# History attention: the reciprocal deviation spread by two single-pass products, and later waits at the history's end

## The chip, the cores and the metric

The kernel runs on one core of a Trainium2 chip. The metric is the device time of one execution in microseconds (us). TensorE multiplies matrices, VectorE (DVE), ScalarE (ACT) and GpSimd (POOL) work elementwise, SyncE (SP) issues the DMAs. Each engine runs its own instruction list in order and waits on semaphores for the others.

## The reference

Two transformer-like layers on x (128 tokens by 256 features). The first block looks at a history of 12544 tokens of 256 features. For each history token it computes

    h  = tok @ hist_W + hist_b              (512 features)
    hn = (h - mean(h)) * rsqrt(var(h) + 1e-5) * g + beta
    e  = gelu(hn)
    logit = gelu(e @ W1 + b1) @ W2 + b2

and then one context vector, the softmax(logit)-weighted sum of e over all tokens. From this vector come 3x3 kernels (one set for each of 16 heads), which are applied to the 128x128 score maps of x. Linear attention, a mixture of experts, a cross attention of x over the same 12544 tokens (keys and values are projections of the history), a retention block and a low-rank feed-forward part follow, one after the other.

## The kernel before, in words

**The history loop.** The 12544 tokens go through in 49 chunks of 256 (`NCH`, `CH`); features lie on partitions, tokens on columns. In one pass of its loop TensorE does, in this order: `project(n, 0)` (12 products of 256 columns), `mean_square(n-1)`, `values_turn(n-1)`, `project(n, 1)` (12 more), `spread_rstd(n-1)`, in odd passes `weight_logit`, `weight_hidden`, and `keys_product(n)` (12 products). The projections split each float32 number in a rounded part and a rest, both of type float32r, and sum three products; such a product is one record in the trace. A product of plain float32 operands is two records.

**The deviation.** The mean over features is taken out by centred weights, so only the variance is missing. ACT squares the 512 projected features, DVE adds them up to 128 partitions (`add_squares`), and `mean_square` (L673) sums the partitions by two products of one column each, whose stationary operand is the 128x128 block of squares. The result has tokens on partitions, two columns. DVE adds epsilon (`variance`, L1555), POOL raises to the power -0.5 (`deviation`, L1478, gives `h_rstd`, 128x2). `spread_rstd` (L681) turns this into a row that all partitions share: two plain float32 products, stationary operand a column of `h_rstd` broadcast to 128x128, moving operand the identity (128 columns). ACT copies the 256 columns out (`widen`, L1238, `rstd_wide`), and DVE's `normalise` (L1570) multiplies by it.

**DVE's order in a pass** (L1612 and after): `keys_parts(n-1)` (waits for ACT's `k_full`), `variance(n-1)`, in even passes `logit`, then from the 17th pass on a wait for POOL's `h_rs` and one `weighted_sum` (L1594), `normalise`, `add_squares(n)`, `normalise`.

**The history's end.** After the last pass DVE finishes the weighted sums and writes the context vector (`cc_wide`). Meanwhile TensorE turns xn (L769) and multiplies it by the query, key and value weights (`qkv0`), then waits for `cc_wide` and does `kg1` (four products of 256 columns and a bias of one row), then the 16 score products (`scores0`, L797), then turns `kg_h` (L803), from which the kernels come. Right behind `cc_wide`, DVE waits until the last key and value stores have landed and sets `history_done` (L1676). Three things wait for that: SP, before it loads `rows0` and the four pieces of FFN weights (L583, L586); ACT, before it copies `kT0` and `v0` (L1330, L1331); and, in order behind it, DVE's own `q_blocks` (L1699). The score products need `q_blocks` and `kT0`. `stay_awake(n, at)` (L756) issues n plain float32 products of the identity with itself into a bank nobody reads.

Of the kernel before, what the change touches and what calls it, by code (L numbers as in the profile page):

```python
# [19 lines left out]
F32 = mybir.dt.float32  # L20
F32R = mybir.dt.float32r
U8 = mybir.dt.uint8
U32 = mybir.dt.uint32
ALU = mybir.AluOpType
# [3 lines left out]
P = 128  # L28
# [12 lines left out]
NCH = S // CH  # L41
HB = CH // 2
# [33 lines left out]
VG = -(-TILES // VT)  # L76
# [29 lines left out]
def wait_at(eng, sem, value):  # L106

    if isinstance(value, int) and value <= 0:
        return
    eng.wait_ge(sem, value)  # L110
# [67 lines left out]
POOL_STEPS = """  # L178
half_power v_ones rstd1 rstd_kg rstd2 rstd_att rstd3 rstd4 turned5 rstd5 rms5 rstd6"""
DVE_STEPS = """  # L180
hist_constants hist_weights x_parts mask var1 xn1 g_shift cc_wide history_done q_blocks0 var_kg kg_n att0_0 att0_1
kg_hT att0_2 att0_3 kern_shift kernels s_max0 s_max2 s_max1 probT0 s_max3 probT1
probT2 s_max4 probT3 probT4 o0 o0T x1 var2 xn2 xT2 v1
kv_blocks var_att gated1 gT x2 var3 xn3 xT3 g_neg hid0 hid1 mixed0 hid2 mixed1 hid3 mixed2 hid4 mixed3 x3 var4
# [81 lines left out]
def build_kernel(nc, k_scratch, v_scratch, ones_scratch, ctx_t, x_in, mask_in, const_in, hist_in, l0_in, rows0_in, xw_in, x_bo_in, x_o_in, l1_in, rows1_in, v_in,  # L266
                 tables_in, out):
    with ExitStack() as outer:
        def sem(name):
            return outer.enter_context(nc.semaphore(name))  # L270

        def sb(name, shape, dt=F32, scope=outer):
            return scope.enter_context(nc.sbuf_tensor(name, shape, dt))


        bank = outer.enter_context(nc.psum_tensor("bank", [P, 8, 512], F32))
# [19 lines left out]
        ident = part(const, CONST_COLS, "ident")  # L296
# [19 lines left out]
        la = ExitStack()  # L316
# [13 lines left out]
        square1 = sb("square1", [P, CH], scope=la)  # L330
        h_var = sb("h_var", [P, 2], scope=la)
        h_rstd = sb("h_rstd", [P, 2], scope=la)
        rstd_wide = sb("rstd_wide", [P, CH], scope=la)
        normed = sb("normed", [P, 2, CT, PW], scope=la)
        eh = sb("eh", [P, 2, CT, GW], scope=la)
# [7 lines left out]
        cc_wide = k_full[:, NCH % 2].rearrange("p m (c t) -> p (m c) t", t=P)  # L343
# [11 lines left out]
        gone = sb("gone", [P, 1], scope=lb)  # L355
# [7 lines left out]
        kg_n = sb("kg_n", [P, D], scope=lb)  # L363
# [97 lines left out]
        ld_const, ld_hist, ld_small = sem("ld_const"), sem("ld_hist"), sem("ld_small")  # L461
# [4 lines left out]
        pe_s = Steps(sem("pe_steps"), PE_STEPS)  # L466
# [5 lines left out]
        h_high, h_low, h_proj, h_sq = sem("h_high"), sem("h_low"), sem("h_proj"), sem("h_sq")  # L472
        h_add2, h_add1, h_ms, h_ve, h_rs = sem("h_add2"), sem("h_add1"), sem("h_ms"), sem("h_ve"), sem("h_rs")
        h_bc, h_rw, h_nm, h_eh = sem("h_bc"), sem("h_rw"), sem("h_nm"), sem("h_eh")
        h_w1, h_hid, h_w2, h_lg = sem("h_w1"), sem("h_hid"), sem("h_w2"), sem("h_lg")
        h_gm, h_p, h_ws = sem("h_gm"), sem("h_p"), sem("h_ws")

# [32 lines left out]
        k_stored = [sem("k_stored0"), sem("k_stored1")]  # L510
        v_stored = [sem("v_stored0"), sem("v_stored1")]
# [131 lines left out]
        def _(pe):  # L643
# [31 lines left out]
                last.then_inc(h_ms, 1)  # L675

            def spread_rstd(n):
                pe.wait_ge(h_rs, n + 1)
                wait_at(pe, h_rw, n)
                for s in range(2):  # L680
                    last = nc.tensor.matmul(bank[:, 4, s * HB:(s + 1) * HB], h_rstd[:, s:s + 1].broadcast_to([P, P]),  # L681
                                            ident, start=True, stop=True)
                last.then_inc(h_bc, 1)

            def weight_hidden(i, part_of):
# [79 lines left out]
            def turn(name_in, src, name_out, at=0, banks=None):  # L765

                dve_s.wait(pe, name_in)
                for k in range(KD):
                    last = nc.tensor.transpose(bank[:, at, k * P:(k + 1) * P], src[:, k * P:(k + 1) * P], ident)  # L769
                pe_s.done(last, name_out)  # L770
# [6 lines left out]

            pe.wait_ge(ld_l0, 16 * L0_PIECES)
            pe.wait_ge(h_nm, CT * NCH)
            turn("xn1", xn, "xn1_t")  # L780
            act_s.wait(pe, "xT1")
            wq, wk, wv = (part(w0, L0_COLS, n, KD) for n in ("x_q", "x_k", "x_v"))
# [4 lines left out]


            pe.wait_ge(ld_kg, 16)
            dve_s.wait(pe, "cc_wide")  # L790
            kg1, kg2 = part(w0, L0_COLS, "kg1", CT), part(w0, L0_COLS, "kg2", KD)
            pe_s.done(product(bank[:, 0, 0:D], [(cc_wide[:, c], kg1[:, c]) for c in range(CT)]
# [3 lines left out]
            for h in range(H):  # L796
                last = nc.tensor.matmul(bank[:, 4 + h // 4, (h % 4) * T:(h % 4 + 1) * T], q_blocks[:, h // 8, h % 8],  # L797
                                        kT[:, h // 8], start=True, stop=True)
# [87 lines left out]
            for m in range(KD):  # L886
                nc.tensor.matmul(bank[:, 5, m * P:(m + 1) * P], k_sig[:, m * P:(m + 1) * P], v_lin[:, m * P:(m + 1) * P],
                                 start=True, stop=True)
# [617 lines left out]
        def _(dve):  # L1506
            V = nc.vector
            own = [0]

            def link(ins):  # L1510

                own[0] += 1
                ins.then_inc(dve_own, 1)
                dve.wait_ge(dve_own, own[0])

            def done(ins, name):

                dve_s.done(ins, name)
                dve_s.wait(dve, name)
# [3 lines left out]
            V.memset(ones[:, :], 1.0).then_inc(dve_own, 1)  # L1523
            V.memset(group_stats[:, :, :], 0.0).then_inc(dve_own, 1)
            own[0] += 3
            done(V.memset(inv_width[:, :], 1.0 / C2), "hist_constants")
            dve.wait_ge(ld_hist, 32)
            link(V.tensor_reduce(w_mean[:, :], w_raw, AX_X, ALU.add))
# [23 lines left out]
            def variance(n):  # L1552
                dve.wait_ge(h_ms, n + 1)
                wait_at(dve, h_rs, n)
                V.tensor_scalar(h_var[:, :], bank[:, 4, CH:CH + 2], LN_EPS, None, ALU.add).then_inc(h_ve, 1)  # L1555

            def add_squares(n):
                dve.wait_ge(h_sq, 2 * n + 2)
# [16 lines left out]
            def logit(i):  # L1575
                group, at, width = group_of(i), i % GP * PW, pair_width(i)
                gb = i // GP % 2
                dve.wait_ge(h_w2, i + 1)
                if i % GP == 0 and i >= 2 * GP:
                    dve.wait_ge(h_ws, pieces_before((i // GP - 1) * GC))  # L1580
                    dve.wait_ge(h_gm, i // GP - 1)
                V.tensor_scalar(logits[:, gb, at:at + width], bank[:, 6, 0:width], v_hist["b2"], None, ALU.add,
                                ALU.max, accum_out=pair_max[:, gb, i % GP:i % GP + 1]).then_inc(h_lg, 1)
                if i == pairs_of(group)[-1]:
                    dve.wait_ge(h_lg, i + 1)
                    V.tensor_reduce(group_stats[:, group, MAX_COL:MAX_COL + 1],
                                    pair_max[:, gb, pairs_of(group)[0] % GP:i % GP + 1], AX_X,
                                    ALU.max, negate=True).then_inc(h_gm, 1)

            def weighted_sum(group, half, c, lo, width):  # L1590
                gb = GROUPS[group][0] // GC % 2
                dve.wait_ge(h_p, group + 1)
                part_of = eh[:, gb, c, lo:lo + width]
                V.tensor_tensor_reduce(part_of, part_of, logits[:, gb, lo:lo + width], 1.0, 0.0, ALU.mult, ALU.add,  # L1594
                                       group_stats[:, group, half * CT + c:half * CT + c + 1]).then_inc(h_ws, 1)
# [19 lines left out]
            for n in range(NCH):  # L1615
                if 0 <= n - 1:
                    keys_parts(n - 1)
                    variance(n - 1)
                if n % 2 == 0 and 0 <= (n - 8) // 2:
                    logit((n - 8) // 2)  # L1620
                group, piece = divmod(n - 2 * GC, GC)
                if 0 <= group:
                    dve.wait_ge(h_rs, n)
                    weighted_sum(group, *pieces_of(group)[piece])
                if 0 <= n - 1:
                    normalise(n - 1, 0)
                add_squares(n)
                if 0 <= n - 1:
                    normalise(n - 1, 1)
                if n == FRONT_SLOT - 1:  # L1630
                    mask_rows()
                if n == FRONT_SLOT:
                    spread_x("var1")
                if n == FRONT_SLOT + 3:
                    spread_x("xn1")
            left = [(STEADY - 1, p) for p in pieces_of(STEADY - 1)[NCH - 2 * GC - GC * (STEADY - 1):]]
            variance(NCH - 1)
            weighted_sum(left[0][0], *left[0][1])
            normalise(NCH - 1, 0)
            normalise(NCH - 1, 1)  # L1640
# [28 lines left out]
            link(V.tensor_reduce(cc[:, :], g_cc[:, :, :].rearrange("p g (h c) -> p c (g h)", c=CT), AX_X, ALU.add))  # L1669
            link(V.tensor_scalar(cc[:, :], cc[:, :], g_one[:, :], None, ALU.mult))  # L1670
            done(V.tensor_copy(cc_wide[:, :, :], cc[:, :].unsqueeze(2).broadcast_to([P, CT, P])), "cc_wide")
            for b in range(2):
                dve.wait_ge(k_stored[b], 32 * ((NCH + 1 - b) // 2))
                dve.wait_ge(v_stored[b], 16 * ((VG + 1 - b) // 2))
            dve.wait_ge(pe_s.sem, 1)
            done(V.memset(gone[:, :], 0.0), "history_done")  # L1676

            def layer_stats(n, src):

# [17 lines left out]
            def head_blocks(out, b, m, name=None):  # L1697

                ins = V.tensor_tensor(out[:, m], b.unsqueeze(1).broadcast_to([P, 8, T]),  # L1699
                                      head_col.unsqueeze(2).broadcast_to([P, 8, T]), ALU.mult)  # L1700
                link(ins) if name is None else done(ins, name)
# [8 lines left out]
            pe_s.wait(dve, "qkv0")  # L1710
            head_blocks(q_blocks, bank[:, 1, 0:T], 0)
            head_blocks(q_blocks, bank[:, 1, T:2 * T], 1, "q_blocks0")
            pe_s.wait(dve, "kg1")
            layer_stats("_kg", bank[:, 0, 0:D])
            link(V.scalar_tensor_tensor(out=kg_n[:, :], in0=bank[:, 0, 0:D], scalar=mv[:, 0:1],
# [355 lines left out]
```

## Time and profile before

| | us |
|---|---|
| three runs | 903.31, 915.29, 939.04 (median 915.29) |
| the profiled execution, its own time | 910.28 |
| its span in the trace | 908.5 |
| granted TensorE clock, mean | 0.969 of full |
| TensorE busy | 849.7 (94%) |
| DVE busy | 630.8 (69%) |
| ACT busy | 549.4 (60%) |
| POOL busy | 104.1 (11%) |

TensorE records overlap (matmuls are pipelined and their ends are modelled), so what a product costs is read from start to start, not from its length. 1.8 us of the profiled execution lie outside the span.

### The profile page before, as it was taken

The page shows a single profiled execution, that of the slowest core. Times are in us where ns is not written, and L with a number is a line of the kernel's source. Part 1 is how long each engine was busy: PE and PEld are TensorE (multiplying, and loading weights), DVE is VectorE, ACT ScalarE, POOL GpSimd, SP SyncE. Part 2 cuts the span into 40 slices and gives each one's busy share as a digit, 9 for nine tenths or more (in the row PEclk, how much of TensorE's full clock was granted, in tenths as well). Part 3 has the DMA queues.
Part 4 walks back from the last instruction along what each step waited for, and adds up shares of the span by engine and source line. Part 5 has one row for each costly group of instructions (what it writes and reads, how often), then busy time and mean ns, then how long its engine had stood idle before and what let it go on. Part 6 is the DMA issues. An engine that isn't in the chain of part 4 may idle for free. (4 is left out here: it accounts for less than half of the span.)

```text
span 908.5 us, 21807 instructions
## 1 busy us (share of the span) xinstructions
PE 849.7 (94%) x8804; PEld 686.6 (76%) x8804; DVE 630.8 (69%) x1289; ACT 549.4 (60%) x952; POOL 104.1 (11%) x116
## 2 busy tenths in 40 slices
PE   3999999999999999968889989999999999999988
PEld 3988888888888888836777853677777777777776
DVE  3555667777767677787964459996799898992242
ACT  2776778787787786872822110665677667778421
POOL 1322222222222222200000000000000000000000
PEclk9999999999999999997989999998899999999988
DMA  3366365546545653528219287478689999925000
GB/s 128 106 171 172 106 181 154 163 123 182 154 140 141 181 133 112 140 70 276 87 21 160 39 190 178 91 144 180 140 191 198 159 214 199 157 77 205 32 1 7
DMA packets 83141, 125.01 MB, mean 138 GB/s; under 512 B 10776, under 2 KB 73498, under 8 KB 82268
## 3 DMA queue, kind: packets, MB, share of 16 engines
q1 hardware_dynamic: 83040, 123.61, 55.3%
q8 instruction: 70, 1.15, 0.6%
q14 instruction: 31, 0.25, 0.1%
HBM read 84.06 MB, written 39.52 MB: 136 GB/s over the span
## 5 line engine op out<-in xcount | busy, mean ns | idle before, releaser
L1413 ACT ACTIVATE prob<-bank 128x1024 f32<-128x1024 f32 (+1 forms) x200 | 190.8, 1005 | 84.3 <-PE bank L1009 83.7
L1905 DVE TENSOR_REDUCE unit_max<-bank 128x1 f32<-128x512 f32 (+1 forms) x350 | 221.2, 675 | 29.3 <-PE bank L985 28.1
L647 PE MATMUL bank<-hc_high,w_high 128*128 128x256 f32 x392 | 115.6, 295 | 8.6 <-POOL hc_low L1473 8.4
L1570 DVE SCALAR_TENSOR_TENSOR normed<-bank,b_centered,rstd_wide 128x256 f32<-128x256 f32 x196 | 85.4, 477 | 48.3 <-ACT rstd_wide L1238 48.3
L1009 PEld LDWEIGHTS bank<-q_stack,k_stack 49*128 49x128 f32 x1568 | 105.4, 192 | 11.4 <-ACT q_stack L1405 3.2
L1024 PE MATMUL bank<-prob,vals 128*32 128x128 f32 x3136 | 111.2, 281 | 2.6 <-issue 2.5
L647 PE MATMUL bank<-hc_high,w_low 128*128 128x256 f32 x392 | 111.0, 283 | 0.0
L647 PE MATMUL bank<-hc_low,w_high 128*128 128x256 f32 x392 | 110.7, 282 | 0.0
L1009 PE MATMUL bank<-q_stack,k_stack 49*128 49x128 f32 x1568 | 105.4, 272 | 2.6 <-ACT q_stack L1405 1.1
L985 PE MATMUL bank<-k_stack,q_max 49*128 49x512 f32 (+1 forms) x400 | 100.9, 498 | 3.2 <-DVE unit_max L1905 2.7
L1024 PEld LDWEIGHTS bank<-prob,vals 128*32 128x32 f32 x3136 | 82.5, 112 | 25.9 <-issue 22.0
L1231 ACT ACTIVATE square<-bank,b_centered 128x256 f32<-128x256 f32 x196 | 81.6, 473 | 25.8 <-PE bank L647 25.8
L696 PE MATMUL bank<-eh,hw 128*128 128x512 f32 (+1 forms) x200 | 92.2, 585 | 0.0
L647 PEld LDWEIGHTS bank<-hc_high,w_high 128*128 128x128 f32 x392 | 74.6, 190 | 9.4 <-issue 9.4
L1223 ACT ACTIVATE eh<-normed,hw 128x512 f32<-128x512 f32 (+1 forms) x100 | 74.9, 807 | 0.0
L647 PEld LDWEIGHTS bank<-hc_high,w_low 128*128 128x128 f32 x392 | 74.9, 191 | 0.0
L647 PEld LDWEIGHTS bank<-hc_low,w_high 128*128 128x128 f32 x392 | 74.5, 190 | 0.0
L647 PE MATMUL bank<-hc_high,x_high 128*128 128x256 f32 x196 | 73.2, 374 | 0.0
L985 PEld LDWEIGHTS bank<-k_stack,q_max 49*128 49x128 f32 x400 | 38.4, 187 | 43.3 <-DVE unit_max L1905 19.7
L1594 DVE CUSTOM_DVE_ANT_0 eh<-eh,logits 128x1024 f32<-128x1024 f32 (+1 forms) x52 | 59.5, 1162 | 14.7 <-POOL h_rstd L1478 12.9
L1473 POOL TENSOR_TENSOR hc_low<-hc_raw,hc_high 128x512 fp32r<-128x512 f32 x49 | 62.5, 1277 | 46.4 <-DVE group_stats L1594 45.2
L1483 POOL TENSOR_TENSOR rstd<-var_eps,half_power 128x1 f32<-128x1 f32 x8 | 4.4, 551 | 506.2 <-DVE var_eps L1682 502.3
(326 smaller groups left out, 1356.2 us busy)
## 6 DMA issues: line engine op xcount, KB each, us to landing
k_stack<-k_scratch SPq DMA_DIRECT2D x336, 112.0 KB, 5.3
vals<-v_scratch SPq DMA_DIRECT2D x8, 1666.0 KB, 8.9
v_scratch<-vst SPq DMA_DIRECT2D x12, 1088.0 KB, 9.3
hc_raw<-in_ctx_t SPq DMA_DIRECT2D x49, 256.0 KB, 3.1
k_scratch<-k_high SPq DMA_DIRECT2D x49, 256.0 KB, 3.4
k_scratch<-k_low SPq DMA_DIRECT2D x49, 256.0 KB, 3.5
w_ffn<-in_l SPq DMA_DIRECT2D x4, 1920.0 KB, 13.1
w_l<-in_l SPq DMA_DIRECT2D x6, 603.0 KB, 5.4
```

The source lines that it names most:

```text
L647: last = nc.tensor.matmul(out_ap, lhs, rhs, start=(n == 0), stop=(n == len(pairs) - 1))
L696: last = nc.tensor.matmul(bank[:, w1_bank(i), 0:width], w1_hist[:, c, :], eh[:, gb, c, at:at + width], start=(c == 0), stop=(c == CT - 1))
L985: last = nc.tensor.matmul(bank[:, at, 0:hi - lo], q_max[head_rows[hh], s, :], k_stack[s % 2][head_rows[hh], lo:hi], start=True, stop=True)
L1009: last = nc.tensor.matmul(bank[:, at + hh, t * T:(t + 1) * T], k_stack[s % 2][head_rows[hh], k * P:(k + 1) * P], q_stack[head_rows[hh], s, ...
L1024: last = nc.tensor.matmul(bank[at:at + 32, SUM_BANK, 0:T], vals[:, s % 2, hh, k * VW:k * VW + 32], prob[:, e % NPB, hh, t * T:(t + 1) * T] ...
L1223: A(eh[:, group % 2, c, at:at + width], normed[:, i % 2, c, 0:width], ACT.Gelu, bias=v_hist["beta"][:, c:c + 1], scale=v_hist["g"][:, c:c ...
L1231: ins = A(square[:, c, :], bank[:, 2 * (n % 2) + half, (c % 2) * CH:(c % 2 + 1) * CH], ACT.Square, bias=b_centered[:, c:c + 1])
L1413: A(prob[:, e % NPB, :, 0:width], bank[:, at:at + 2, 0:width], ACT.Exp).then_inc(c_exp, 1)
L1473: TT(hc_low[:, b], hc_raw[:, b], hc_high[:, b].bitcast(F32), ALU.subtract).then_inc(h_low, 1)
L1570: V.scalar_tensor_tensor(out=normed[:, n // 2 % 2, c, at:at + CH], in0=bank[:, 2 * b + half, (c % 2) * CH:(c % 2 + 1) * CH], scalar=b_cent ...
L1594: V.tensor_tensor_reduce(part_of, part_of, logits[:, gb, lo:lo + width], 1.0, 0.0, ALU.mult, ALU.add, group_stats[:, group, half * CT + c: ...
L1905: V.tensor_reduce(unit_max[:, s % 2, u, hh:hh + 1], bank[:, at[hh], 0:width], AX_X, ALU.max, negate=True).then_inc(c_red, 1)
```

## The change

The deviation is split like the projections' operands: DVE rounds `h_rstd` to float32r (`rstd_parts[:, 0]`), subtracts this from `h_rstd` (`rstd_parts[:, 1]`), and `spread_rstd` does four float32r products in place of two float32 ones. The identity is copied once into a float32r tile. The wait for POOL on DVE moves from the front of the weighted sum into `deviation_parts`, which every pass now has. TensorE gets four and eight `stay_awake` products at the history's end, and `history_done`, with its waits, stands behind `q_blocks`.

```diff
+        rstd_parts = sb("rstd_parts", [P, 2, 2], F32R, scope=la)
+        ident_r = sb("ident_r", [P, P], F32R, scope=la)
...
             def spread_rstd(n):
-                pe.wait_ge(h_rs, n + 1)
+                pe.wait_ge(h_rl, n + 1)
                 wait_at(pe, h_rw, n)
                 for s in range(2):
-                    last = nc.tensor.matmul(bank[:, 4, s * HB:(s + 1) * HB], h_rstd[:, s:s + 1].broadcast_to([P, P]),
-                                            ident, start=True, stop=True)
+                    for part_of in range(2):
+                        last = nc.tensor.matmul(bank[:, 4, s * HB:(s + 1) * HB],
+                                                rstd_parts[:, part_of, s:s + 1].broadcast_to([P, P]),
+                                                ident_r[:, :], start=(part_of == 0), stop=(part_of == 1))
                 last.then_inc(h_bc, 1)
...
             pe.wait_ge(h_nm, CT * NCH)
+            stay_awake(4, 4)
             turn("xn1", xn, "xn1_t")
...
             pe.wait_ge(ld_kg, 16)
+            stay_awake(8, 4)
             dve_s.wait(pe, "cc_wide")
...
+            dve.wait_ge(ld_const, 16)
+            link(V.tensor_copy(ident_r[:, :], ident))
             done(V.memset(inv_width[:, :], 1.0 / C2), "hist_constants")
...
+            def deviation_parts(n):
+                dve.wait_ge(h_rs, n + 1)
+                wait_at(dve, h_bc, n)
+                V.tensor_copy(rstd_parts[:, 0, :], h_rstd[:, :]).then_inc(h_rh, 1)
+                dve.wait_ge(h_rh, n + 1)
+                V.tensor_tensor(rstd_parts[:, 1, :], h_rstd[:, :], rstd_parts[:, 0, :].bitcast(F32),
+                                ALU.subtract).then_inc(h_rl, 1)
...
                     logit((n - 8) // 2)
+                if 0 <= n - 1:
+                    deviation_parts(n - 1)
                 group, piece = divmod(n - 2 * GC, GC)
                 if 0 <= group:
-                    dve.wait_ge(h_rs, n)
                     weighted_sum(group, *pieces_of(group)[piece])
...
             variance(NCH - 1)
+            deviation_parts(NCH - 1)
             weighted_sum(left[0][0], *left[0][1])
...
             done(V.tensor_copy(cc_wide[:, :, :], cc[:, :].unsqueeze(2).broadcast_to([P, CT, P])), "cc_wide")
-            for b in range(2):
-                dve.wait_ge(k_stored[b], 32 * ((NCH + 1 - b) // 2))
-                dve.wait_ge(v_stored[b], 16 * ((VG + 1 - b) // 2))
-            dve.wait_ge(pe_s.sem, 1)
-            done(V.memset(gone[:, :], 0.0), "history_done")
...
             head_blocks(q_blocks, bank[:, 1, T:2 * T], 1, "q_blocks0")
+            for b in range(2):
+                dve.wait_ge(k_stored[b], 32 * ((NCH + 1 - b) // 2))
+                dve.wait_ge(v_stored[b], 16 * ((VG + 1 - b) // 2))
+            dve.wait_ge(pe_s.sem, 1)
+            done(V.memset(gone[:, :], 0.0), "history_done")
```

## Rows read from the trace of the kernel before

**Rows 1.** The page, part 1: busy time, share of span, instructions of each engine.
```profile
PE 849.7 (94%) x8804; PEld 686.6 (76%) x8804; DVE 630.8 (69%) x1289; ACT 549.4 (60%) x952; POOL 104.1 (11%) x116
```
**Rows 2.** Windows: stretch, its length, busy us (instructions) by engine, granted clock, DMA.
```profile
180.00:220.00 40.00, 40.00 (x282) 34.26 (x281) 28.97 (x65) 33.75 (x67) 10.54 (x11) 1.00 0.59 161
415.00:420.00 5.00, 4.11 (x9) 2.95 (x10) 3.18 (x6) 1.94 (x3) 0.00 (x0) 0.52 0.59 198
420.00:425.00 5.00, 5.00 (x22) 4.35 (x22) 3.01 (x9) 1.70 (x2) 0.55 (x1) 0.50 1.02 436
627.00:644.00 17.00, 17.00 (x192) 13.46 (x193) 7.93 (x13) 5.82 (x6) 0.00 (x0) 0.50 0.55 102
```
**Rows 3.** Timeline, TensorE in one pass: start us, length us, engine, line, tiles, records.
```profile
202.14 0.50 PE L673 MATMUL bank<-inv_width,square 128*128 128x1 f32 x4
202.50 0.63 PE L722 MATMUL bank<-const,k_full 128*128 128x128 f32 x4
...
204.29 0.28 PE L647 MATMUL bank<-hc_low,w_high 128*128 128x256 f32 x1
204.41 0.60 PE L681 MATMUL bank<-const,h_rstd 128*128 128x128 f32 x4
204.85 1.02 PE L705 MATMUL bank<-hidden,w_wide 128*128 128x512 f32 x2
```
**Rows 4.** Timeline, TensorE in the cross attention, float32r products.
```profile
602.86 0.50 PE L985 MATMUL bank<-k_stack,q_max 49*128 49x512 f32 x2
603.20 1.00 PE L1009 MATMUL bank<-q_stack,k_stack 49*128 49x128 f32 x16
604.22 0.49 PE L985 MATMUL bank<-k_stack,q_max 49*128 49x512 f32 x2
```
**Rows 5.** Timeline, POOL and TensorE's weight loads, the same pass as rows 3.
```profile
203.09 0.69 POOL L1478 TENSOR_TENSOR h_rstd<-h_var,half_power 128x2 f32<-128x2 f32 x1 [3.53 <-DVE h_var L1555]
204.30 0.52 PEld L681 LDWEIGHTS bank<-const,h_rstd 128*128 128x128 f32 x4
```
**Rows 6.** Timeline, the same two steps in passes 5, 24 and the last.
```profile
49.97 0.69 POOL L1478 TENSOR_TENSOR h_rstd<-h_var,half_power 128x2 f32<-128x2 f32 x1 [4.15 <-DVE h_var L1555]
50.72 0.18 PEld L681 LDWEIGHTS bank<-const,h_rstd 128*128 128x128 f32 x1
...
196.19 0.69 POOL L1478 TENSOR_TENSOR h_rstd<-h_var,half_power 128x2 f32<-128x2 f32 x1 [5.16 <-DVE h_var L1555]
197.00 0.19 PEld L681 LDWEIGHTS bank<-const,h_rstd 128*128 128x128 f32 x1
...
388.51 0.18 PEld L681 LDWEIGHTS bank<-const,h_rstd 128*128 128x128 f32 x1 [0.83 <-POOL h_rstd L1478]
```
**Rows 7.** Timeline, DVE: two small operations that depend on each other.
```profile
412.40 0.17 DVE L1661 TENSOR_TENSOR g_sum<-g_w,group_stats 128x8 f32<-128x8 f32 x1
412.60 0.16 DVE L1662 TENSOR_REDUCE g_one<-g_sum 128x1 f32<-128x8 f32 x1
```
**Rows 8.** Timeline, TensorE at the history's end.
```profile
411.88 1.03 PE L647 MATMUL bank<-w_l,xT 128*128 128x256 f32 x4
415.89 3.75 PE L647 MATMUL bank<-w_l,k_full 128*128 128x256 f32 x8 [2.98 <-DVE gone L1676]
...
420.72 6.09 PE L797 MATMUL bank<-kT,q_blocks 128*128 128x128 f32 x32
426.65 0.38 PE L803 MATMUL bank<-const,kg_h 128*128 128x128 f32 x2
```
**Rows 9.** Timeline, DVE: the query blocks at the history's end.
```profile
415.90 2.48 DVE L1699 TENSOR_TENSOR q_blocks<-bank,const 128x1024 f32<-128x1024 f32 x2
```
**Rows 10.** Timeline, ACT's copy of the keys, same stretch.
```profile
415.96 0.38 ACT L1330 ACTIVATE kT<-bank 128x256 f32<-128x256 f32 x1 [7.67 <-DVE gone L1676]
```
**Rows 11.** Timeline, SP: the last value stores are issued.
```profile
403.21 3.00 SPq L558 DMA_DIRECT2D v_scratch<-vst  x2
```
**Rows 12.** Waits of the DMA queue: engine, line, waited for, us in total.
```profile
SPq L611 <- DVE x L1797: 55.2, 1, 55.2
```

More of the change, by code:

```diff
@@ L180 @@
 DVE_STEPS = """
-hist_constants hist_weights x_parts mask var1 xn1 g_shift cc_wide history_done q_blocks0 var_kg kg_n att0_0 att0_1
+hist_constants hist_weights x_parts mask var1 xn1 g_shift cc_wide q_blocks0 history_done var_kg kg_n att0_0 att0_1
 kg_hT att0_2 att0_3 kern_shift kernels s_max0 s_max2 s_max1 probT0 s_max3 probT1
@@ L474, in build_kernel @@
         h_bc, h_rw, h_nm, h_eh = sem("h_bc"), sem("h_rw"), sem("h_nm"), sem("h_eh")
+        h_rh, h_rl = sem("h_rh"), sem("h_rl")
         h_w1, h_hid, h_w2, h_lg = sem("h_w1"), sem("h_hid"), sem("h_w2"), sem("h_lg")
```

## The prediction

> **What bounds the kernel now.** I read the page's totals first: TensorE is busy 94% of the span, DVE 69%, ACT 60% [rows 1]. An average over stages decides nothing, so the windows come next. In the middle of the history loop TensorE is busy 40.00 of 40.00 us at full clock (1.00, the 2.4 GHz level), while ACT has 33.75, DVE 28.97 and POOL 10.54 [rows 2]. The loop, some 365 of 908.5 us, is therefore worth what TensorE's own work is worth, and a wait put in front of TensorE there costs its full length unless it ends before TensorE arrives. Third, the timeline of one pass, for what each step costs from start to start [rows 3], and beside it when POOL delivers the deviation and when TensorE loads it [rows 5, 6]. Fourth, the history's end: the granted clock is 0.52 and 0.50 in the two stretches in which TensorE does `kg1` and the score products [rows 2], after it had stood idle 2.98 us [rows 8].
>
> **The spread's products.** Before: two float32 products, four records, from 204.41 to the next step at 204.85, so 0.44 us a pass [rows 3]. After: four float32r products, each a record with its own 128x128 weight load. Again four loads and four records; only the columns streamed under each load are halved. What such a load costs alone is shown twice. The four records of `mean_square` stream a single column each and yet take 202.50 - 202.14 = 0.36 us, 0.09 each [rows 3]. And the 16 float32r products of 128 columns in the cross attention take 604.22 - 603.20 = 1.02 us [rows 4]. They run in pairs on the two halves of the rows: the two products of 512 columns ahead of them take 0.34 us together, where 1024 columns in a row at 2.4 GHz would need 0.43. So eight pairs take 0.127 us each, though 128 columns stream in 0.053. Both say that the weight load, not the columns, sets the pace, at 0.09 to 0.127 us. Four: 0.36 to 0.51 us against 0.44. The neighbouring float32r products of 256 columns, 0.12 each (204.29 to 204.41) [rows 3], give 0.48. I take **0** as the term, in the middle; bounds 49 x (-0.08) = -3.9 and 49 x 0.07 = +3.4 us. If the columns alone counted, four would take 0.21 us and the term would be 49 x (-0.23) = -11.3; that end is a rival.
> The Trainium skill has rules for both sides, in "TensorE: Matmul & The Clock Gate". Its section on the back-to-back issue gap gives N / 2.4 + 2.5 ns, 56 ns at 128 columns; by that the term would be 49 x (0.22 - 0.44) = -10.8 us. Its section on LDWEIGHTS gives P / 1.2, 107 ns for 128 weight columns whatever the rows; by that the term is 49 x (0.43 - 0.44), about nothing. The rows above agree with the second.
>
> **The new step between POOL and TensorE.** POOL ends 203.09 + 0.69 = 203.78, TensorE's load starts 204.30: slack 0.52 us [rows 5]. Now DVE stands between. A hop from one engine to the next is 0.06 (POOL ends 50.66, the load that waits for it starts 50.72) [rows 6]. A small DVE operation and its dependent successor start 0.20 apart, and one lasts 0.17 [rows 7]. So 0.06 + 0.20 + 0.17 + 0.06 = 0.49 us: it fits into 0.52, with 0.03 to spare. In 38 of 49 passes I find the slack at 0.45 to 0.53 and cost the step at nothing there; the cover is POOL's early end, and if the step is 0.1 longer it costs 38 x 0.07 = 2.7 us. In the other passes POOL is late. Four passes at the start are like 49.97: slack 0.06, so +0.43 each, 1.7 us. Five passes, eight apart, are like 196.19 (slack 197.00 - 196.88 = 0.12; the first of them 0.07): +0.38 each, 1.9 us. In the last pass DVE's weighted sum used to run beside POOL, whose operation took so long that TensorE idled 0.83 us [rows 6]; now the weighted sum is queued behind the parts, POOL runs alone, and I take -0.2 (bounds -0.8 and +0.4). Sum: **+3.4**. Bounds: small operations of 0.1 us each give +1.5; of 0.25 each (0.62 for the whole step) give 38 x 0.10 + 9 x 0.53 = +8.6.
> Queued behind the new wait on DVE are the weighted sum and `normalise`. In passes from the 17th on DVE waited for the same POOL event already, so the sum starts 0.4 later; `normalise` waits for TensorE and ACT anyway and DVE has 11 us in 40 free [rows 2]. In earlier passes the next thing is `normalise`, which comes after the spread in any case. Nothing. POOL's next low part waits for the weighted sum, 0.4 us later, against some 2 us before TensorE needs it: nothing.
>
> **The start.** The copy of the identity waits for the first DMA, and everything behind it waits for the second and third on the same queue. Nothing; if the constants came last, one copy, at most 0.3 us.
>
> **The history's end.** The four first `stay_awake` products fall into the idle time ahead of `qkv0`: 8 records of 0.11 us [rows 3], nothing. The other eight (16 records, 1.8 us) fall into the 2.98 us of idle time ahead of `kg1` [rows 8] and leave 1.2. TensorE had been busy up to 412.9 before that gap, and the clock fell in it; with the gap 1.2 I expect it to hold. Then `kg1` takes half of 420.72 - 415.89 = 4.83, so 2.4 us, to 418.3. The 16 score products are 32 records of 0.111, so 3.55 us instead of 426.65 - 420.72 = 5.93 [rows 8].
> What is late next is `kT0`: `history_done` now stands behind `q_blocks`, which end at 415.90 + 2.48 = 418.38 [rows 9]; the memset and two hops, then ACT's 0.38 [rows 10], and the scores start at 418.95 rather than 418.3. They end at 422.5 instead of 426.65: **-4.15**. The kernels, the taps and all that follows hang on the turn of `kg_h` behind the scores, so this is carried on; if DVE's kernel steps cannot follow, part is lost. With the clock fallen all the same, the move of `history_done` is hidden (`kg1` ends at 420.7, `kT0` at 418.9): 0. In an execution that had the full clock there before, the move costs up to 0.7. Bounds -4.5 and +0.7.
> The stores that `history_done` waits for are issued from 403.21 on [rows 11] and had landed, since `kT` starts right behind the memset [rows 10]. SP's loads of `rows0` and FFN weights start 2.6 us later; SP then waits 55.2 us for x1 [rows 12], so nothing.
>
> **Sum.** 0 + 3.4 - 4.15 = -0.8 us against the profiled execution's 910.28 (span 908.5 and 1.8 around it): **909.5**. The three runs' median is 915.29, 5 us above this execution; they range over 36 us, and 2% of the median (18.3 us) is about what a measurement of this kernel tells from no change.
>
> **The rivals.**
> *Slower: DVE's step is too long in every pass.* The place is the 0.52 us between POOL and the load, and it decides from 0.03 us above my 0.49. At 0.62 it costs 8.6; at 0.75, if rounding two columns were slower than rows 7, 38 x 0.23 + 9 x 0.66 = 14.7, with the end's gain 920.8. Against it: the operations touch two columns each. Chance 0.15, time 914 to 921.
> *The product is priced by its columns* (the page's gap rule): 909.5 - 11.3 = 898.2, if the waits do not grow with it. For it: half the columns; against it: [rows 3, 4]. Chance 0.12.
> *The end gives nothing:* the clock falls anyway, or falls elsewhere instead. 17 us at half clock stand at 627 to 644 [rows 2]; such a stretch costs up to 8.5, and where it falls is not of this change's making. 909.5 + 4.2 = 913.7, to 918. Chance 0.15.
>
> **How the numbers follow.** The forecast (909.5, own range 903 to 915) has 0.58. The range goes down to 898 for the column rival and up to 921 for the two slower ones and for runs like the middle one before. Faster than 897 needs the column price and a clock stretch less: 0.06. Slower than 933.6 needs the long step and a bad clock together: 0.04. Within 2%: 0.90.
>
> **What would show it.** L681: four records still about 0.44 us start to start (0.22 would be the column rival). The load of L681 in a middle pass still directly behind the last projection, with the second part ready under 0.1 us before. Pass length in the middle unchanged. The clock at `kg1` and the scores 1.00 instead of 0.50, and L797 ending about 4 us sooner after `cc_wide`. Wrong I would be by a float32r load that is cheaper than those of rows 4, or by TensorE idle ahead of L681 in every pass.

## The result: about 1.8% slower, the loss in the first fifteen passes

Over twenty runs each the changed kernel takes 919.99 us in the median (913.12 to 933.27), the kernel before 915.05 (897.82 to 941.40). The medians differ by 4.9 us. The ratio is 1.0176, with a 95% interval of 1.0138 to 1.0215, about 16 us more. It is taken over the fast runs alone, those of each kernel within 1.5% of its fastest, since half-clock stretches lengthen the others. I had forecast 0.8 us less.

The profiled execution took 913.12 us (span 911.0), only 2.8 more than the one of before. That hides the loss: behind its first convolution tap the changed execution is 11.4 us shorter (466.0 against 477.4), in stages that the change does not touch. The one of before spent 17 us at half clock at 627 to 644 [rows 2], the changed one has no such stretch there. What the change did is read from the stages that it touches. The first `mean_square` starts at 23.28 us before and at 23.46 after; the copy that writes `cc_wide` starts at 415.31 and at 433.19; the first convolution tap at 431.12 and at 445.01. The rows, first of the kernel before, then of the kernel after (`cc_wide` lies in the memory of `k_full` and has its name in the trace):

```profile
23.28 0.50 PE L673 MATMUL bank<-inv_width,square 128*128 128x1 f32 x4
415.31 0.43 DVE L1671 COPY k_full<-cc 128x512 f32<-128x512 f32 x1
431.12 0.87 DVE L1749 TENSOR_SCALAR conv<-att,kern 128x128 f32<-128x128 f32 x4
...
23.46 0.50 PE L676 MATMUL bank<-inv_width,square 128*128 128x1 f32 x4
433.19 0.43 DVE L1690 COPY k_full<-cc 128x512 f32<-128x512 f32 x1
445.01 0.87 DVE L1768 TENSOR_SCALAR conv<-att,kern 128x128 f32<-128x128 f32 x4
```

So:

| from | before | after | difference |
|---|---|---|---|
| first `mean_square` to `cc_wide` (the loop and its tail) | 392.03 | 409.73 | +17.70 |
| `cc_wide` to the first tap (the history's end) | 15.81 | 11.82 | -3.99 |
| sum | 407.84 | 421.55 | +13.71 |

The windows (stretch, length, busy us and instructions of PE, PEld, DVE, ACT, POOL, clock, DMA) of the kernel after say where in the loop:

```profile
60.00:100.00 40.00, 36.94 (x256) 31.16 (x254) 25.78 (x56) 25.44 (x53) 9.32 (x10) 1.00 0.60 159
180.00:220.00 40.00, 39.99 (x281) 34.04 (x280) 31.10 (x74) 31.99 (x64) 9.80 (x10) 1.00 0.52 149
```

In the middle TensorE is full, as before [rows 2]. Early on it idles 3.06 of 40 us, in a stretch in which it was busy throughout before. The waits between 25 and 140 us (engine, tile, line, what it waited for; us in total, times, longest) name the reason:

```profile
PEld bank L685 <- DVE rstd_parts L1571: 15.7, 14, 1.6
```

And the timeline of DVE around the sixth deviation of the kernel after, then of POOL, then of TensorE's weight loads:

```profile
64.27 1.28 DVE L1569 CAST rstd_parts<-h_rstd 128x2 fp32r<-128x2 f32 x1 [0.80 <-POOL h_rstd L1485]
65.59 0.16 DVE L1571 TENSOR_TENSOR rstd_parts<-h_rstd,rstd_parts 128x2 fp32r<-128x2 f32 x1
...
63.55 0.69 POOL L1485 TENSOR_TENSOR h_rstd<-h_var,half_power 128x2 f32<-128x2 f32 x1 [6.35 <-DVE h_var L1564]
64.25 1.28 POOL L1480 TENSOR_TENSOR hc_low<-hc_raw,hc_high 128x512 fp32r<-128x512 f32 x1
...
65.80 0.52 PEld L685 LDWEIGHTS bank<-ident_r,rstd_parts 128*128 128x128 f32 x4 [0.97 <-DVE rstd_parts L1571]
```

The rounding of two columns lasts 1.28 us and ends within 0.02 us of POOL's low part (the subtraction that makes `hc_low`), which had started 0.02 before it. TensorE's load comes 1.56 us after POOL's deviation, where it used to come 0.52 after [rows 5]. In a later pass (the 25th deviation) the same three steps:

```profile
221.40 0.17 DVE L1569 CAST rstd_parts<-h_rstd 128x2 fp32r<-128x2 f32 x1 [0.80 <-POOL h_rstd L1485]
221.60 0.16 DVE L1571 TENSOR_TENSOR rstd_parts<-h_rstd,rstd_parts 128x2 fp32r<-128x2 f32 x1
...
221.89 0.53 PEld L685 LDWEIGHTS bank<-ident_r,rstd_parts 128*128 128x128 f32 x4
```

The rounding lasts 0.17 us, TensorE waits for nothing. The reason lies in the order: from the 17th pass on POOL's low part also waits for DVE's weighted sum (`h_ws`), which stands behind the two operations. Before that nothing holds it back, and it starts the moment the deviation is done. The line's spread in the kernel after, shortest, median and longest in ns of 49:

```profile
L1569 DVE CAST rstd_parts<-h_rstd x49: 169/171/1283, 25.1 to 405.8; 128x2 fp32r<-128x2 f32 x49
```

Counted over all passes, the rounding lasts 1.22 to 1.28 us in the first 15 and 0.17 in the other 34. What each pass adds is read from the start of the spread's first load, counted from the first `mean_square` and compared with the kernel before: 1.01 to 1.06 us in eleven of the first fifteen passes, 1.39 in each of the four in which POOL is late as well, together 16.9; then 0.33 once and 0.28 four times in the passes that I had named; 0.5 less in the last pass. The passes between are about 0.01 us shorter each, some 0.2 in all, and 0.15 is added behind the last spread. That is the 17.7.

The products, and the history's end, in the kernel after:

```profile
206.28 0.56 PE L685 MATMUL bank<-ident_r,rstd_parts 128*128 128x128 f32 x4
206.68 1.07 PE L710 MATMUL bank<-hidden,w_wide 128*128 128x512 f32 x2
207.59 1.88 PE L701 MATMUL bank<-eh,hw 128*128 128x512 f32 x4
```

```profile
431.50 2.36 PE L764 MATMUL bank<-const 128*128 128x128 f32 x16
433.69 1.98 PE L650 MATMUL bank<-w_l,k_full 128*128 128x256 f32 x8
435.60 0.69 PE L650 MATMUL bank<-rows_kg,ones_row 1*128 1x256 f32 x2
436.89 3.81 PE L804 MATMUL bank<-kT,q_blocks 128*128 128x128 f32 x32 [0.59 <-ACT kT L1337]
440.53 0.38 PE L810 MATMUL bank<-const,kg_h 128*128 128x128 f32 x2
```

The windows of the same stretch:

```profile
430.00:435.00 5.00, 5.00 (x26) 4.50 (x26) 4.69 (x19) 0.00 (x0) 0.00 (x0) 0.77 0.24 8
435.00:440.00 5.00, 4.41 (x34) 3.68 (x33) 4.17 (x11) 3.43 (x5) 0.55 (x1) 1.00 0.50 160
```

Four records in 0.40 us where 0.44 stood, but a whole pass became only 0.01 us shorter (from one `mean_square` to the next, 204.02 to 212.16, it is 8.14; before, 202.14 to 210.29, 8.15). The step behind the spread takes back what the spread gives: it lasts 0.91 us to its successor (206.68 to 207.59), before 0.86 (204.85 to 205.71), so that the two together take 1.31 against 1.30.

At the end the eight `stay_awake` products (431.50) keep TensorE busy up to `kg1` (433.69). The granted clock is 0.77 over 430 to 435 (0.50 in 430.0 to 431.5, 1.00 in 432.4 to 433.6) and 1.00 under the scores, instead of 0.50; `kT0` is the last to come (0.59 us of idle time). The turn of `kg_h` starts 440.53 - 433.19 = 7.3 us behind `cc_wide` instead of 426.65 - 415.31 = 11.3.

### The profile page after: what moved, and what is told of

The parts are those of the page before. It is cut to its first block and busy times, and to the rows that moved or that the text cites. A ratio compares the mean times of both kernels' runs of the same rounds, so it can differ in the third digit from the quotient of the medians.

```text
span 911.0 us, 21968 instructions
## 1 busy us (share of the span) xinstructions
PE 844.5 (93%) x8828; PEld 681.8 (75%) x8828; DVE 669.2 (73%) x1388; ACT 549.0 (60%) x952; POOL 103.1 (11%) x116
## 5 line engine op out<-in xcount | busy, mean ns | idle before, releaser
L1016 PEld LDWEIGHTS bank<-q_stack,k_stack 49*128 49x128 f32 x1568 | 102.5, 187 | 12.1 <-issue 3.3
L1031 PE MATMUL bank<-prob,vals 128*32 128x128 f32 x3136 | 106.2, 276 | 0.0
L1016 PE MATMUL bank<-q_stack,k_stack 49*128 49x128 f32 x1568 | 103.1, 268 | 3.3 <-ACT q_stack L1412 1.1
L1031 PEld LDWEIGHTS bank<-prob,vals 128*32 128x32 f32 x3136 | 79.6, 109 | 21.4 <-issue 19.4
L701 PEld LDWEIGHTS bank<-eh,hw 128*128 128x128 f32 x200 | 35.9, 190 | 34.3 <-issue 33.2
L1260 ACT ACTIVATE k_full<-bank,x_wts 128x256 f32<-128x256 f32 x98 | 40.9, 468 | 32.4 <-PE bank L650 30.7
## 6 DMA issues: line engine op xcount, KB each, us to landing
w_ffn<-in_l SPq DMA_DIRECT2D x4, 1920.0 KB, 14.7
```

Source lines behind the costliest of these rows:

```text
L701: last = nc.tensor.matmul(bank[:, w1_bank(i), 0:width], w1_hist[:, c, :], eh[:, gb, c, at:at + width], start=(c == 0), stop=(c == CT - 1))
L1016: last = nc.tensor.matmul(bank[:, at + hh, t * T:(t + 1) * T], k_stack[s % 2][head_rows[hh], k * P:(k + 1) * P], q_stack[head_rows[hh], s, ...
L1031: last = nc.tensor.matmul(bank[at:at + 32, SUM_BANK, 0:T], vals[:, s % 2, hh, k * VW:k * VW + 32], prob[:, e % NPB, hh, t * T:(t + 1) * T] ...
L1260: ins = A(k_full[:, n % 2, m, :], bank[:, 7, m * CH:(m + 1) * CH], ACT.Identity, bias=xb[:, m:m + 1])
```

## The experiments

Theory: DVE's rounding collides with POOL's low part in the first 15 passes, and TensorE waits for it. Rivals: the two operations or the float32r products are slow of themselves early on; the history's end, not the spread, costs the time; DVE's own delay costs it, not TensorE's wait. Four kernels shared a chip, then four another; "loop" is from the first `mean_square` to `cc_wide`, "end" from there to the first tap, both of one profiled execution. The loops of the kernel before and of e2, which runs the same loop, are 0.05 us apart, so tenths can be read there. The ratios are rougher: e1's rests on three runs of it, e5's on five.

| kernel | loop us | end us | ratio to before (95%) |
|---|---|---|---|
| before | 392.03 | 15.81 | |
| changed | 409.73 | 11.82 | 1.0176 (1.0138 to 1.0215) |
| e1 spread alone | 409.65 | 13.41 | 1.0245 (1.0176 to 1.0315) |
| e2 end alone | 392.08 | 11.81 | 1.0007 (0.9960 to 1.0055) |
| e3 low part later | 395.06 | 11.82 | 1.0001 (0.9957 to 1.0045) |
| e4 old products | 410.18 | 11.81 | one run |
| e5 one product | 380.62 | 11.82 | 0.9742 (0.9632 to 0.9851) |
| e6 reduce | 406.64 | 11.82 | one run |
| e7 low part later, all | 394.18 | 11.82 | 0.9894 (0.9819 to 0.9968) |
| e8 parts unused | 391.63 | 11.82 | one run |

**e1 and e2: the halves alone.** e1 is the changed kernel with the history's end of before, e2 the kernel before with the new end.

> The spread's change alone; the history's end as before. Theory A (collision): in the first 15 passes DVE's rounding of the deviation runs beside POOL's low part and lasts 1.28 us, so the context vector is written 17.9 us later than before (433.2 instead of 415.3 in the traces at hand) and nothing is given back: 932 to 936 for a profile like the changed one, ratio to before 1.018 to 1.021. Theory B (the end's move costs): the context vector would come on time within 3 us and the ratio would be 1.00 to 1.005.

> The end's change alone (twelve more products, the later wait); the spread as before. Theory A: the context vector at 415.3 within 0.5 us, the first convolution tap 11.8 us behind it instead of 15.8 (clock full in the scores), so 4 us less in an execution whose clock fell there, ratio 0.994 to 0.999. Theory B: slower than before, ratio 1.01 or more, with the time lost behind the context vector.

The spread alone makes the loop as long as in the changed kernel (409.65), and its ratio, 1.0245, is the highest (its interval holds the 1.018 to 1.021 expected); the end alone leaves the loop as it was and makes the end 4.0 us shorter. Theory A holds, B falls. e1's own end took 13.41 us, not 15.81: the clock stood at half only in a part of it that time, so the end's 4 us are a gain over the one profiled execution and less over another. The eight kernels with the new end all take 11.81 or 11.82. e2's ratio, 1.0007, does not show the gain: it lies above the 0.994 to 0.999 expected, and its interval reaches down to 0.996. No run has the `stay_awake` products without the later `history_done`, or the other way round; which of the two gives how much is argued from the timeline, not shown.

**e3: POOL's low part behind the parts.**

```diff
                 wait_at(pool, h_ws, n - 2 * GC)
+                if n < 2 * GC:
+                    wait_at(pool, h_rl, n - 1)
                 TT(hc_low[:, b], hc_raw[:, b], hc_high[:, b].bitcast(F32), ALU.subtract).then_inc(h_low, 1)
```

> The changed kernel, but in the first 16 passes POOL starts its low part only when DVE has made both parts of the deviation. Theory A: the rounding lasts 0.17 us in every pass, passes 5 to 14 lose nothing, the first five about 0.4 us each; the context vector at 418.5 to 419.5, ratio to before 0.995 to 1.002. Rival (the step itself is too long early on, whatever POOL does, or the two operations are slow because of the float32r type): the rounding stays at 1.28 us and the context vector at 433.

The timeline of DVE, POOL and the weight loads around the seventh deviation of e3:

```profile
67.38 0.17 DVE L1571 CAST rstd_parts<-h_rstd 128x2 fp32r<-128x2 f32 x1 [0.80 <-POOL h_rstd L1487]
67.58 0.16 DVE L1573 TENSOR_TENSOR rstd_parts<-h_rstd,rstd_parts 128x2 fp32r<-128x2 f32 x1
...
67.88 1.27 POOL L1482 TENSOR_TENSOR hc_low<-hc_raw,hc_high 128x512 fp32r<-128x512 f32 x1 [0.54 <-DVE rstd_parts L1573]
...
67.87 0.53 PEld L685 LDWEIGHTS bank<-ident_r,rstd_parts 128*128 128x128 f32 x4
```

The rounding is back at 0.17 us and the loop gets back 14.7 of the 17.7 us. Neither the two operations nor their float32r type are slow of themselves. `cc_wide` came at 419.56, just outside the 418.5 to 419.5 expected: its first `mean_square` was 1.0 us later than in the changed kernel, and for one deviation, the fifteenth, the rounding still lasted 1.29 us, since my condition leaves out the low part that runs beside it.

**e7: one pass more.** The condition is `n <= 2 * GC`.

> As e3, with POOL's low part held back in one more pass, the fifteenth, which still had a rounding of 1.29 us there. The context vector 1.0 us sooner after the first mean square than in e3 (394.0 against 395.06; the kernel before 392.0, the changed kernel 409.7); ratio to before 0.995 to 1.002.

394.18 against the 394.0 expected. One collision less is worth 0.9 us, which also prices a single one. What is left over the kernel before, 2.1 us, comes from the passes in which POOL is late: 0.35 in each of the first four, 0.33 and four times 0.28 later; the last pass gives 0.5 back, the drift of the others some 0.2. The ratio, 0.9894, came out lower than the range expected and lower than e2's, though e7's loop is 2.1 us longer than e2's; the runs do not resolve such amounts, and I rest nothing on them.

**e4: the old products under the new waits.**

```diff
                 for s in range(2):
-                    for part_of in range(2):
-                        last = nc.tensor.matmul(bank[:, 4, s * HB:(s + 1) * HB],
-                                                rstd_parts[:, part_of, s:s + 1].broadcast_to([P, P]),
-                                                ident_r[:, :], start=(part_of == 0), stop=(part_of == 1))
+                    last = nc.tensor.matmul(bank[:, 4, s * HB:(s + 1) * HB], h_rstd[:, s:s + 1].broadcast_to([P, P]),
+                                            ident, start=True, stop=True)
```

> The changed kernel with DVE's two operations and all waits kept, but TensorE spreads the unrounded deviation by the two float32 products of before. Theory A: the context vector where the changed kernel has it, 433 within 1.5 us, since the products cost the same (0.44 against 0.40 to 0.44 us a pass); if the columns set the price of a product it comes 8 us or more later than the changed kernel's.

The loop is 0.45 us longer than with the four float32r products, 0.01 us a pass (`cc_wide` came at 434.95, at the edge of the 1.5 us allowed, with a first `mean_square` 1.3 us later). The change of format is worth next to nothing here.

**e5: half the weight loads.** POOL writes `h_rstd` as float32r, and each half is one product with `ident_r`; no step on DVE, the new end.

> The end's change, no step on DVE, and POOL writes the deviation rounded to float32r; TensorE spreads it by one float32r product a half. The rest of the deviation is left out, so it is less exact. If the weight load sets a product's price (as in the rows of the kernel before), two loads instead of four: 0.22 us less in each of 49 passes, the context vector 10.5 to 11 us sooner after the first mean square than in the kernel before (381 instead of 392), ratio 0.983 to 0.99. If the columns set it, 0.33 us less a pass: 16 us.

TensorE at the 25th deviation of e5:

```profile
198.75 0.33 PE L682 MATMUL bank<-ident_r,h_rstd 128*128 128x128 f32 x2
198.92 1.07 PE L706 MATMUL bank<-hidden,w_wide 128*128 128x512 f32 x2
```

Two records from 198.75 to 198.92, 0.17 us. The loop is 11.4 us shorter than before, 0.23 a pass. That is the loads' price (0.22 expected), not the columns' (0.33). Every record has its own load, so the runs do not tell the load from another fixed cost of a record. The ratio, 0.9742 (0.9632 to 0.9851), is below the 0.983 to 0.99 expected; the 11.4 us of the loop and the 4.0 of the end make 15.4, or 0.983, and the rest I cannot assign. This is the one version whose loop is shorter than in both kernels by more than 1 us. It gives up the rest of the deviation, so it is a trade of exactness for time, which the changed kernel did not make.

**e6: another operation for the rounding.**

```diff
-                V.tensor_copy(rstd_parts[:, 0, :], h_rstd[:, :]).then_inc(h_rh, 1)
+                V.tensor_reduce(rstd_parts[:, 0, :], h_rstd[:, :].unsqueeze(2), AX_X, ALU.max).then_inc(h_rh, 1)
```

> The changed kernel, with the rounding done by a maximum over one element (a reduce with one operand) in place of a copy. If only operations that use DVE's second read path are stopped by POOL, the reduce lasts about 0.17 us in the first passes and the subtraction behind it, with its two operands, takes the 1.1 us instead; the context vector at the same place, 433. If every DVE operation is stopped, the reduce lasts 1.28. If it is the copy alone, both are short and the context vector comes at 418 to 420.

DVE and POOL around the sixth deviation of e6:

```profile
63.14 0.16 DVE L1569 TENSOR_REDUCE rstd_parts<-h_rstd 128x2 fp32r<-128x2 f32 x1 [0.80 <-POOL h_rstd L1485]
63.33 1.09 DVE L1571 TENSOR_TENSOR rstd_parts<-h_rstd,rstd_parts 128x2 fp32r<-128x2 f32 x1
...
63.12 1.28 POOL L1480 TENSOR_TENSOR hc_low<-hc_raw,hc_high 128x512 fp32r<-128x512 f32 x1
```

The reduce, started 0.02 us behind POOL's operation, takes its usual 0.16 us; the subtraction, with two operands in SBUF, is held in its place, and ends together with POOL's (64.42 and 64.40). So it is not DVE as a whole that is held, but the copy and the two-operand operation. The loop is 3.1 us shorter than the changed kernel's, since the reduce's 0.2 us pass under POOL; `cc_wide` came at 430.0, not at the 433 I had written.

**e8: the collision without TensorE's wait.** The products and the wait are those of before (`pe.wait_ge(h_rs, n + 1)`); DVE makes both parts all the same, and nobody uses them. POOL gets one wait more (`wait_at(pool, h_rl, n)`), so that it does not overwrite a deviation that DVE has still to read.

> The changed kernel, in which DVE still makes both parts and collides with POOL, but TensorE waits for POOL's result and spreads that by the two float32 products of before, so that the parts are not used. If the loss comes by TensorE's wait for the parts, the context vector is back at 392 us after the first mean square, within 2 us, though the rounding still lasts 1.28 us in the first passes. If DVE's own delay (normalise and all behind it) were the cause, it stays at 405 or more.

DVE, POOL and the weight loads around the seventh deviation of e8:

```profile
65.94 1.27 DVE L1568 CAST rstd_parts<-h_rstd 128x2 fp32r<-128x2 f32 x1 [0.80 <-POOL h_rstd L1484]
...
65.90 1.29 POOL L1478 TENSOR_TENSOR hc_low<-hc_raw,hc_high 128x512 fp32r<-128x512 f32 x1
...
66.42 0.53 PEld L684 LDWEIGHTS bank<-const,h_rstd 128*128 128x128 f32 x4
```

The collision is there in full, 1.27 us, and the loop takes 391.63 us, 0.4 less than before. DVE has the time; the loss is TensorE's wait for what DVE makes. The late passes cost nothing either, so the whole cost of the new step is this one wait.

## Why the prediction was wrong, step by step

- **The spread's products, 0:** right. 0.45 us over 49 passes (e4), and two loads less give 0.23 us a pass (e5). The rival by columns is out.
- **The new step between POOL and TensorE, +3.4: this failed; it cost 17.7.** "So 0.06 + 0.20 + 0.17 + 0.06 = 0.49 us: it fits into 0.52" is measured as 0.45 in later passes (POOL's deviation to a load that may start, with the copy 0.04 behind POOL, 0.20 to the subtraction, 0.16, and 0.05), and it fits. But I went on: "In 38 of 49 passes I find the slack at 0.45 to 0.53 and cost the step at nothing there". (They are 39; 38, 4, 5 and 1 make only 48 passes.) Eleven of them cost 1.01 to 1.06 us each, and the four early ones with POOL late 1.39 instead of 0.43. What was wrong is the 0.20 from the rounding to the subtraction: beside POOL's low part it is 1.25 to 1.32, since the rounding lasts 1.22 to 1.28. I priced the two operations by rows of the history's end, where POOL is idle. What POOL does at the moment they run was in the trace and unread: at the seventh deviation of the kernel before its low part starts right behind,

```profile
64.07 0.69 POOL L1478 TENSOR_TENSOR h_rstd<-h_var,half_power 128x2 f32<-128x2 f32 x1 [5.32 <-DVE h_var L1555]
64.76 1.28 POOL L1473 TENSOR_TENSOR hc_low<-hc_raw,hc_high 128x512 fp32r<-128x512 f32 x1
```

  while DVE had nothing to do then. "In earlier passes the next thing is `normalise`, which comes after the spread in any case. Nothing" looked behind the new wait only, not beside it. I even used the sign of such a collision: the last pass, in which POOL's operation "took so long" beside DVE's weighted sum that TensorE idled 0.83 us [rows 6]; it lasted 1.60 us there instead of 0.69:

```profile
386.69 1.22 DVE L1594 CUSTOM_DVE_ANT_0 eh<-eh,logits 128x1024 f32<-128x1024 f32 x1
386.85 1.60 POOL L1478 TENSOR_TENSOR h_rstd<-h_var,half_power 128x2 f32<-128x2 f32 x1 [4.61 <-DVE h_var L1555]
```

- **The five late passes and the last:** right in kind. 0.33 once and 0.28 four times, 1.45 us where I had 1.9; the last pass 0.5 less rather than 0.2. Without the collision the loop costs 2.1 us (e7), where I had 3.4.
- **The history's end, -4.15:** right against this one execution, -3.99, with `kT0` as the thing that is late next (0.59 us of idle time). The clock did not simply hold over a gap of 1.2 us, as I had written: it was at half (0.50) up to the start of the eight products, there was no gap ahead of `kg1`, and it was full (1.00 from 432.4 on) before `kg1` began. That the size fits is in part luck: e1, with the old end, took 1.6 us more there than the new end, not 4.0. The first four `stay_awake` products kept nothing awake (0.55 in 425 to 430). Of the later load of the FFN weights I see no cost: in e2 the stretch from the first tap to the end is 474.9 us, before 477.4, though with half-clock stretches that differ.
- **Slower rival:** its place, the gap between POOL and the load, was right, and its sign. Its mechanism was not: no step that is too long in every pass, but one that POOL holds in fifteen passes and leaves alone in the others. With 17.7 us less 4.0 it comes to 910.28 + 13.7 = 924.0, above the 914 to 921 that I had written for it. That the median of the changed kernel, 919.99, lies in that range, and within my outer bounds of 898 to 921, is luck with the half-clock stretches.

The Trainium skill has the rule that I did not draw on: "GPSIMD Engine Reference", Key points, says that GpSimd shares its SBUF interfaces with VectorE, with contention against DVE instructions in a 2-port perf mode or with two SBUF inputs. By that rule the trace agrees in e6: the subtraction with two inputs takes 1.09 us, the one-operand reduce 0.16. Whether the copy runs in such a mode the page does not say; the runs show only that it is held.

Open: why the step behind the spread takes 0.05 us longer when the spread takes 0.04 less. And the medians and ratios hold a part I cannot assign, since half-clock stretches fall differently in each execution (e2 to e7).

## What to carry to other kernels

Before a small operation goes between two engines, look at what a third one does in that very slot, in the first passes too, where pipelines are not yet held back by each other; a mean or a middle pass does not show it. Operations of 0.17 us are priced by the neighbour that can stop them, not by themselves. And a product with a fresh 128-column weight block was priced here by its load, or by something else that each record pays: halving the columns gave nothing, halving the records did.

## What the runs showed of the hardware

- A DVE copy of 128x2 elements that starts 0.02 to 0.08 us after a two-operand POOL operation ends with it, within 0.03 us (1.22 to 1.28 us instead of 0.17), in all 15 passes where they meet. A two-operand DVE subtraction likewise (1.02 to 1.09 instead of 0.16). A reduce with one operand does not (0.16). The DVE operation is held; POOL's stays at 1.26 to 1.28.
- The other way round, POOL's power of two columns, started 0.16 us behind DVE's weighted sum, lasted 1.60 us instead of 0.69 (last pass of the kernel before).
- With 128 weight columns and 128 moving columns four float32r products and two float32 ones cost TensorE the same within 0.01 us a pass; two float32r products cost 0.23 us less.
